# Channel attention, attention and a mixture of LoRA experts in one kernel: the tie test, the two features and the gates change engines

## The reference, cut to what matters

```python
# x: (16, 64, 2048); ctx_4096: (16, 1601, 2048)
x = x + xattn(layernorm(x), ctx_4096, conv_w, gamma, beta)
x = x + attn(layernorm(x), wq, wk, wv, wo)          # causal, 64 tokens, 32 heads, 8 KV heads
x = x + ffn(layernorm(x), gate_w, base_w, base_b, lora_A, lora_B)

def xattn(x, channel_map, ...):      # the part that the change touches
    k = 38                           # of C = 64 channels of x
    # top_k of channel_map over its 1601 channels, at each of the 16 x 2048 places;
    # the mask keeps those of the winners whose index is under 64
    mask = zeros(B, L, C).at[b, l, topk_idx].set(1)
    top, rest = mask * x, (1 - mask) * x
    c_max, c_avg = max(top, C), mean(top, C) * C / k
    s_max, s_avg = max(rest, C), mean(rest, C) * C / (C - k)
    A1 = sigmoid(relu(norm(conv7([c_max, c_avg]))))   # norm over all places, one channel
    A2 = sigmoid(relu(norm(conv7([s_max, s_avg]))))
    return top * A1 + rest * A2
```

## Time and profile before

| | |
|---|---|
| median of 3 runs | 2323.5 us (2322.08 to 2328.86) |
| the profiled execution | 2331.43 us, of which its span is 2329.6 |
| busy in the span | PE 2017.3 (87%), PEld 1656.8 (71%), DVE 1423.9 (61%), ACT 1011.1 (43%), POOL 979.4 (42%) |
| DMA | 407.69 MB, mean 175 GB/s |
| the costliest lines | L1744 to L1746 PE 742.5, 727.5 and 727.3; L1198 POOL 653.8; L440 DVE 521.7; L680 PE 462.7; L641 ACT 416.6 |

### The profile page before, as it was taken

How to read it: one execution, slowest core, us unless ns; L and a number is a source line. 1 busy time by engine, 2 the same in 40 slices (tenths; PEclk the granted TensorE clock), 3 DMA queues, 4 the chain that set the end, 5 groups by cost and what they waited for, 6 DMA issues and landing times. The chain is left out here.

```text
span 2329.6 us, 39066 instructions
## 1 busy us (share of the span) xinstructions
PE 2017.3 (87%) x15210; PEld 1656.8 (71%) x15210; DVE 1423.9 (61%) x2320; ACT 1011.1 (43%) x2006; POOL 979.4 (42%) x866
## 2 busy tenths in 40 slices
PE   4777788677762946999999999999999999999999
PEld 4566565566662935777787888887778878877887
DVE  6999899999999989744444530144445525731111
ACT  7777777777760136432332332232223322422222
POOL 1221121222214531665564555556555435634554
PEclk9999899999985968999999999999999999999999
DMA  9999787899960104542225443322244446333443
GB/s 381 369 359 326 273 302 268 299 327 336 336 215 17 73 19 127 158 127 82 76 84 181 136 142 116 100 80 76 82 152 143 136 127 214 124 109 124 144 144 119
DMA packets 150088, 407.69 MB, mean 175 GB/s; under 512 B 15376, under 2 KB 36112, under 8 KB 148112
## 3 DMA queue, kind: packets, MB, share of 16 engines
q1 hardware_dynamic: 149616, 403.55, 51.0%
q0 software_dynamic: 288, 1.64, 0.2%
HBM read 379.96 MB, written 25.17 MB: 174 GB/s over the span
## 5 line engine op out<-in xcount | busy, mean ns | idle before, releaser
L1198 POOL TENSOR_TENSOR t<-t,t 128x512 fp32r<-128x512 f32 (+1 forms) x488 | 653.8, 1351 | 680.9 <-ACT t L1191 680.5
L1744 PE MATMUL ps<-t,t 128*128 128x512 f32 x1856 | 742.5, 400 | 19.7 <-POOL t L1198 9.5
L1745 PE MATMUL ps<-t,t 128*128 128x512 f32 x1856 | 727.5, 392 | 0.0
L1746 PE MATMUL ps<-t,t 128*128 128x512 f32 x1856 | 727.3, 392 | 0.0
L680 PE MATMUL ps<-t,t 128*128 128x128 bf16 (+1 forms) x6656 | 462.7, 226 | 199.9 <-DVE t L440 185.3
L680 PEld LDWEIGHTS ps<-t,t 128*128 128x128 bf16 x6656 | 405.1, 103 | 292.8 <-DVE t L440 250.3
L1191 ACT ACTIVATE t<-t 128x512 fp32r<-128x512 f32 (+1 forms) x488 | 295.8, 608 | 712.4 <-PE ps L1746 393.1
L440 DVE TENSOR_SCALAR t<-t,t 128x1601 bf16<-128x1601 f32 x512 | 521.7, 1063 | 3.8 <-PE ps L680 0.3
L641 ACT ACTIVATE t<-t,t 128x1601 bf16<-128x1601 f32 x256 | 416.6, 1627 | 74.1 <-DVE t L582 70.6
L1744 PEld LDWEIGHTS ps<-t,t 128*128 128x128 f32 x1856 | 350.9, 189 | 100.2 <-issue 13.2
L1746 PEld LDWEIGHTS ps<-t,t 128*128 128x128 f32 x1856 | 351.1, 189 | 75.2
(11 more groups left out here) (212 smaller groups left out, 1684.2 us busy)
## 6 DMA issues: line engine op xcount, KB each, us to landing
t<-ctxT SPq DMA_DIRECT2D x256, 800.5 KB, 6.2
t<-wqkv SPq DMA_DIRECT2D x192, 256.0 KB, 3.2
t<-wo SPq DMA_DIRECT2D x128, 256.0 KB, 4.6
t<-wb SPq DMA_DIRECT2D x128, 256.0 KB, 3.4
t<-xT SPq DMA_DIRECT2D x32, 256.0 KB, 7.0
t<-xT SPq DMA_DIRECT2D x2, 4096.0 KB, 12.2
t<-x1d SPq DMA_DIRECT2D x32, 256.0 KB, 4.8
x2d<-t SPq DMA_DIRECT2D x32, 256.0 KB, 2.0
```

The costliest lines, as they stand in the source:

```text
L1198: e.tensor_tensor(wlo[r][:, 0:nk, :], raw[r][:, 0:nk, :], wh[r][:, 0:nk, :].bitcast(F32), ALU.subtract).then_inc(w_lo, 1)
L1744: e.matmul(bank[:, :], wh[r][:, q, :], xl, start=(kt == 0), stop=False)
L1745: e.matmul(bank[:, :], wlo[r][:, q, :], xh, start=False, stop=False)
L1746: m = e.matmul(bank[:, :], wh[r][:, q, :], xh, start=False, stop=(c == NCH[p] - 1 and q == nk - 1))
```

## The change

1. **Ties.** The two neighbour comparisons per quad leave VectorE. GpSimd subtracts neighbours instead, one instruction of 28 elements for a quad (`quad_gpsimd`), queued behind its copy of the quad's last tile. The flag is then "the smallest difference is zero" (`fin_vector` step 8 takes a minimum, `flags_vector` step 2 compares with zero). VectorE's `copy_predicated` and step 8 wait for GpSimd's `tied`.
2. **The layernorm's reciprocal** goes from the first to the late call of `ln0_vector` in its round.
3. **Setup.** The warming instruction of GpSimd is a `tensor_tensor` and no longer a `partition_all_reduce`; the gate weights land in another buffer, and GpSimd's copies don't wait for `gate_lo`.
4. **`ln0_out_gpsimd`**, the first six: they wait until the last mask of the search is written.
5. **Statistics.** `LAG` is 3 and no longer 4. The maxima are written straight into the padded feature tile `Yp`. The sums of batches 12 to 14 go from VectorE to TensorE: eight matmuls of 384 columns (eight channels x 48 rows of places) behind the 64 of batches 0 to 7, and one VectorE reduction over the eight. Batch 15 stays on VectorE. ScalarE takes the sums of batches 0 to 7 out of PSUM.
6. **Convolution and gates.** ScalarE writes the scaled top average and the two edges, VectorE the rest average; the centre tap (3) comes first. The relu and a Sigmoid are done on ScalarE, which writes `A2` itself; VectorE is left with the scale and one subtraction.

The diff, cut to its core (unused semaphores and renamed buffers left out):

```diff
 def setup_gpsimd(e):
-    e.partition_all_reduce(fl2[:, 0:2], fl2[:, 2:4], 128, ReduceOp.max).then_inc(warm, 1)
+    e.tensor_tensor(fl2[:, 2:4], fl2[:, 0:2], fl2[:, 0:2], ALU.subtract)
...
 def ln0_vector(e, i, late):
-            if i == LN0_VAR[h] + 1 and not late:
+            if i == LN0_VAR[h] + 1 and late:
                 e.wait_ge(ln0_std, h + 1)
                 e.reciprocal(ln0_rs[h][:, :], Mn[:, :]).then_inc(ln0_rstd, 1)
...
 def bounds(half):
-    e.tensor_tensor(eqb[y][:, two, :], v8[:, y, two, 0:7], v8[:, y, two, 1:8], ALU.is_equal).then_inc(tied, 1)
...
+def quad_gpsimd(e, i):
+    e.wait_ge(maxed, 4 * i + 4)
+    e.tensor_tensor(eqb[y][:, four, :], v8[:, y, four, 0:7], v8[:, y, four, 1:8], ALU.subtract).then_inc(tied, 1)
...
 def rows_gpsimd(e):
     gather_gpsimd(e, 0, d_first[0])
+    e.wait_ge(masked, NMASKS)
     for j in range(6):
         ln0_out_gpsimd(e, j)
...
-    LAG = 4
-    BY_ACT, BY_DVE = range(8, 12), range(12, 16)
+    LAG = 3
+    BY_ACT, BY_PE, BY_DVE = range(8, 12), range(12, 15), range(15, 16)
+    late_sums = ps[4][:, 0:8 * NT * len(BY_PE)].rearrange("p (c n) -> p c n", c=8)
...
 def stats_vector(e):
         for b in range(B - LAG, B):
-            total(b)
+            if b in BY_DVE:
+                total(b)
             rest(b)
+        e.wait_ge(sums8, 2)
+        e.tensor_reduce(row_sums[:, 12:15, :], over_t(late_sums), AX.X, ALU.add).then_inc(v_sums, 1)
...
 def stats_tensor(e):
+        e.wait_ge(crucial, BY_PE.stop)
+        src = crc16[:, BY_PE.start - HB:BY_PE.stop - HB, :, :].rearrange("p b t c -> p c b t")
+        for k in range(8):
+            m = e.matmul(late_sums.rearrange("p c (b t) -> p c b t", t=NT), ident, src[:, 8 * k:8 * k + 8], start=(k == 0), stop=(k == 7))
...
 def conv_vector(e):
-        for s in range(2):
-            do(e.tensor_scalar(Z[:, s, :], Z[:, s, :], sc[:, 12 + s:13 + s], w16[:, 14:15], ALU.mult, ALU.mult))
-        do(e.tensor_scalar(Z[:, :, :], Z[:, :, :], w16[:, 15:16], 0.0, ALU.add, ALU.max))
-        e.wait_ge(z_exp, 1)
-        do(e.tensor_scalar(Zt[:, :, :], Zt[:, :, :], 1.0, None, ALU.add))
-        do(e.reciprocal(A12[:, :, :], Zt[:, :, :]))
-        do(e.tensor_tensor(Dm, A12[:, 0, :], A12[:, 1, :], ALU.subtract))
-        e.tensor_copy(A2, A12[:, 1, :]).then_inc(gates, 1)
+        e.tensor_scalar(sc[:, 14:16], sc[:, 12:14], w16[:, 14:15], None, ALU.mult).then_inc(z_scale, 1)
+        e.wait_ge(z_out, 4)
+        e.tensor_tensor(Dm, A1[:, :, :], A2, ALU.subtract).then_inc(gates, 1)
...
 def conv_scalar(e):
+        e.activation(feature[2], row_sums, ACT.Copy, scale=PART[0]).then_inc(f_in, 1)
+        for x_, cols in ((0, slice(0, 3)), (1, slice(19, 22))):
+            e.wait_ge(conv_edges, x_ + 1)
+            e.activation(Yp[:, :, cols], edge[x_], ACT.Copy).then_inc(f_edge, 1)
...
+            e.activation(Zt[:, s, :], Z[:, s, :], ACT.Relu, scale=sc[:, 14 + s:15 + s], bias=w16[:, 15:16]).then_inc(z_out, 1)
+            e.activation((A1[:, :, :], A2)[s], Zt[:, s, :], ACT.Sigmoid).then_inc(z_out, 1)
```

More of the change, by code:

```diff
@@ L259, in build @@
     crc_off = 96 * KB
-    crc = [at(crc_off + i * 4 * KB, [NT, C]) for i in range(HB, B)]
+    crc16 = at(crc_off + HB * 4 * KB, [B - HB, NT, C])
     crc8 = at(crc_off, [HB, NT, C])
@@ L468, in fin_vector @@
             if s == 8:
-                i = e.tensor_reduce(flg[:, b, :], eqb[y][:, :, :], AX.X, ALU.max)
+                e.wait_ge(tied, 4 * (b + 1))
+                i = e.tensor_reduce(flg[:, b, :], eqb[y][:, :, :], AX.X, ALU.min)
             i.then_inc(fin, 1)
@@ L596, in search_vector @@
                 e.wait_ge(a_dec, g + 1)
-                e.wait_ge(tied, 2 * g + 2)
+                e.wait_ge(tied, g + 1)
                 w = insA[:, 4 * g:4 * g + 4].rearrange("p (a n) -> p a n", n=1).to_broadcast([128, 4, 3])
@@ L661, in search_scalar @@
                         counts_scalar(e, i, v)
+    def quad_gpsimd(e, i):
+        b, t0 = tile_of(4 * i)
+        y, four = b % 2, slice(t0, t0 + 4)
+        if b >= 2 and t0 == 0:
+            e.wait_ge(fin, NF * (b - 1))
+        e.wait_ge(maxed, 4 * i + 4)
+        e.tensor_tensor(eqb[y][:, four, :], v8[:, y, four, 0:7], v8[:, y, four, 1:8], ALU.subtract).then_inc(tied, 1)
     def search_gpsimd(e):
-        e.wait_ge(gate_lo, 1)
         for n in range(B * NT):
@@ L835, in build @@
     crucial, rest_set, rest_max = sem("crucial"), sem("rest_set"), sem("rest_max")
-    crucial_sum, sums8, v_sums = sem("crucial_sum"), sem("sums8"), sem("v_sums")
-    LAG = 4
-    BY_ACT, BY_DVE = range(8, 12), range(12, 16)
+    crucial_sum, sums8, v_sums, top_max = sem("crucial_sum"), sem("sums8"), sem("v_sums"), sem("top_max")
+    LAG = 3
+    BY_ACT, BY_PE, BY_DVE = range(8, 12), range(12, 15), range(15, 16)
+    sums_out = sem("sums_out")
+    feature = [Yp[:, B * f:B * f + B, 3:19] for f in range(4)]
+    row_sums = stat[:, 2, :, :]
+    late_sums = ps[4][:, 0:8 * NT * len(BY_PE)].rearrange("p (c n) -> p c n", c=8)
     def xn_of(b):
@@ L862, in stats_vector @@
             e.wait_ge(crucial, b + 1)
-            e.tensor_reduce(stat[:, 0, b, :], crc_of(b), AX.X, ALU.max)
+            e.tensor_reduce(feature[0][:, b, :], crc_of(b), AX.X, ALU.max).then_inc(top_max, 1)
             if b >= LAG:
@@ new lines, in conv_vector @@
+        e.wait_ge(z_out, 4)
+        e.tensor_tensor(Dm, A1[:, :, :], A2, ALU.subtract).then_inc(gates, 1)
+    def conv_tensor(e):
+        e.wait_ge(f_in, 2)
+        e.wait_ge(rest_max, B)
+        e.wait_ge(top_max, B)
+        e.matmul(edge[0], cst[:, C_SHL:C_SHL + 128], Yp[:, :, 16:19], start=True, stop=True).then_inc(conv_edges, 1)
+        e.matmul(edge[1], cst[:, C_SHR:C_SHR + 128], Yp[:, :, 3:6], start=True, stop=True).then_inc(conv_edges, 1)
+        e.wait_ge(z_part, 1)
+        e.wait_ge(f_edge, 2)
@@ L969, in build @@
+        for s in range(2):
+            e.wait_ge(z_out, s + 1)
+            e.activation((A1[:, :, :], A2)[s], Zt[:, s, :].rearrange("p (b t) -> p b t", t=NT), ACT.Sigmoid).then_inc(z_out, 1)
     row_gates, row_gates_v, gated = sem("row_gates"), sem("row_gates_v"), sem("gated")
```

108 lines of the change are left out of this document (54 added, 54 removed).

## The result

The changed kernel takes 2313.6 us, the median of 11 runs (2308.41 to 2317.76). The kernel before, run beside it, takes 2322.8 us (11 runs, 2319.43 to 2328.86). The ratio is 0.9959 with an interval of 0.9948 to 0.997: 9.2 us faster, between 7 and 12. The forecast was 2310, in a range of 2299 to 2321, with faster as the likeliest. That is 13.7 us under the kernel before where 9.2 were measured. The profiled execution took 2312.61 us, span 2310.4.

A forecast was written before the change was run, and what follows sets the result against it. VectorE was taken to pace the search, the DMA its first 100 us, and TensorE all from 918 us. -8 + 1.3 - 5.7 + 4.9 - 6.2 = -13.7 us gave 2310 against the median, range 2299 to 2321.

The forecast's parts named there:

- the forecast case: Whole kernel: the main outcome, forecast at 2310 us with its own range 2305 to 2315; chance 0.50.
- ties, with GpSimd's part: Search: two short VectorE instructions fewer per quad, -8 us; GpSimd's 64 small differences cost 1.3 us.
- reciprocal: Search: masks ahead of the reciprocal remove both VectorE waits for ScalarE's square root, 5.7 us less; bounds 4.9 and 5.7.
- end of the search: Last masks: freed of GpSimd's products, 8.4 us, partly lent as `fin_vector` instructions are held; net 2.5 us less, bounds 2.5 to 8.4.
- row of sums to feature: TensorE's late sums: wide matmuls add 10.5 us; convolution starts 4.9 us later, with the 2.5 us saved earlier already included.
- feature to gates: Convolution and gates: shorter work on VectorE and ScalarE saves 6.2 us in sum; bounds 4 and 7.
- part 3: Setup at the kernel's start: gains nothing, since the start is bound by the transfer.
- Nothing holds `fin_vector`: Rival, end of the search: the last masks give 8.4 us and not 2.5, total 2304 us; chance 0.12.
- Wide matmuls at 0.117: Rival, late sums: TensorE's wide matmuls run at 0.117 us per 128 columns, total 2305 us; chance 0.12.
- DMA takes the ties' gain: Rival, search: the DMA takes back the 8 us of the ties' removal, total 2318 us; chance 0.15.
- GpSimd's port: Rival, search: each of 64 small differences holds a mask by a fixed time; at 0.35 us, total 2331; chance 0.07.
- The pick waits for `tied`: Rival, search: GpSimd's difference comes late, stuck behind a copy, so VectorE's pick waits; chance 0.01.

The follow-up runs named there:

- e_ties_dve: The changed kernel with the two tie comparisons per quad back on VectorE and GpSimd's differences gone: 2320.84 us, ratio 0.9992 to the kernel before.
- e_recip_early: The changed kernel with the layernorm's reciprocal back ahead of the first masks of its round: 2316.25 us, ratio 0.9972 to the kernel before.
- the first profile: The kernel before, unchanged, in the profiled execution from which the forecast was made: 2331.43 us.
- e_before_again: The kernel before, unchanged, run once more for a second profile: 2325.16 us in the profiled execution.
- e_no_mask_wait: The changed kernel without the wait for the last mask in front of GpSimd's first six products: 2323.55 us, ratio 1.0008 to the kernel before.
- e_wide_consecutive: The changed kernel with the wide matmuls' moving operand read as consecutive elements (sums of batches 12 to 14 not the reference's): 2310.69 us, one run.
- e_ties_four: The changed kernel with four 28-element differences per quad on GpSimd instead of one, 192 more: 2313.84 us, ratio 0.9955 to the kernel before.

## Why the prediction was right, and where it was off

The steps all went the ways that were forecast, by the mechanisms that were forecast save for the reciprocal's, and 2313.6 us lies inside the forecast case's own range of 2305 to 2315. But of the 13.7 us forecast only 9.2 came (7 to 12), and that the total is this near is in part luck: the reciprocal and the end of the search gave up to 4.8 us less than forecast, the ties and the gates about 2 more. By the steps, in us:

| step | forecast | measured |
|---|---|---|
| ties, with GpSimd's part | -6.7 | -8.3 in the trace, -7.2 by medians (e_ties_dve) |
| reciprocal | -5.7 | -2.7 (e_recip_early) |
| end of the search | -2.5 | -2.7 against the first profile, -0.7 against the second |
| row of sums to feature | +7.4 | +7.8 and +7.6 |
| feature to gates | -6.2 | -6.9 in both |
| sum | -13.7 | -12.8, and -11.0 |

The sums are those of the column with the first and the second profile's terms. The medians say -9.2 (7 to 12). In the traces TensorE's last stage starts at 906.2 against 917.8 and 919.0. That is 11.6 and 12.8 earlier, 2 to 4 us more than the medians; the same search ended over a spread of 3 us, which is as much. No run takes part 6 back: the 6.9 of the gates rest on the rows of one stage, alike against both profiles.

**The ties.** Right in size, with a term too many. GpSimd's differences cost some 0.4 us at most, so the 1.3 us charged for them is too much. I had said that the first 100 us would give nothing, as the DMA bounds them; but the changed kernel is 2 us ahead already in round 12, at 124.2 us against 126.2 and 126.9. The DMA share is 1.01 there, at 388 GB/s where it was 384 and, in e_before_again, 383: the tiles came a little sooner. Whether the faster VectorE brought that about isn't settled, since other executions with GpSimd's differences reach that round at up to 126.0, and e_ties_dve without them at 126.3.

**The reciprocal.** This is the step that was mis-sized: 5.7 forecast with bounds of 4.9 and 5.7, and 2.7 measured. Both waits vanished, as the prediction said, but it took it that nothing is late next. Late next is ScalarE's readout L651, queued behind the same square root: 1.84, 0.69 and 0.42 us at the picks of rounds 25, 26 and 37. I asked what lies ahead of the reciprocal on VectorE, and not what lies behind the square root on ScalarE. The waits for TensorE's counts, in rounds 15 to 18 and 27 to 30, are no part of this: they were there before, at 5.7 us, and are 6.3 now.

**The last masks.** Three `fin_vector` instructions were held as forecast, and the net against the first profile is 2.7. But the bounds of 2.5 to 8.4 left out what the second profile shows: the kernel before pays less when GpSimd's load of code ends later against the masks, and then the gain is 0.7. On the other side stands what e_no_mask_wait showed. Setup's instruction, "nothing" in part 3, removes the load of code (e_ties_dve shows it gone) that had kept the products away from the small picks; part 4's wait takes over that service. Part 3 without part 4 loses the 10 us again, and in the first profile of the kernel before the last small pick (702.99 to 703.17) was clear of the products (703.70) by 0.5 us.

**Late sums.** 16 x 384 x 1.72 ns = 10.5 us is what the trace shows, to the hundredth; the reduction was 0.56 and not 0.6, and the feature starts 0.56 us behind it. e_wide_consecutive shows that choosing the row by its step was what made it right: L881 and L1143 have the same type and shape, and only their steps differ.

**Convolution and gates.** 20.5 us against the 21 forecast. The Sigmoid starts 0.02 us after its table load ends (853.12 + 1.28, then 854.42), as the square root had the earlier trace rows. The drain that the Trainium skill, "ScalarE: Activation LUTs", on what ACT_TABLE_LOAD costs, adds to the load is in neither row.

**The rivals.** Nothing holds `fin_vector`: refuted, 2.27 us each. Wide matmuls at 0.117: refuted (10.50 us). DMA takes the ties' gain: refuted, waits of 15.4 against 15.7 us, and e_ties_dve is 7.2 us slower. GpSimd's port: refuted by e_ties_four with the fourfold, at 1.2 us for 192 more. The pick waits for `tied`: no such wait in the trace.

## What to carry to other kernels

When a wait is taken away, look at the queue of the engine that was waited for: whatever stands behind the awaited instruction there is as late as before, and the next reader of it inherits the wait. Before work is put on an engine "that is idle", add it to the end of its own row: TensorE had 3.8 us of slack for 10.5 us of matmuls, and taking them off again gave 6.6 us. An instruction of another engine that only warmed something up may be what kept two engines out of each other's way; if it goes, say what keeps the order now.

## What was not expected of the hardware

- VectorE's masks and small GpSimd instructions share without loss to VectorE: 28 elements took GpSimd 0.23 us at least and mostly about 1.0 in e_ties_four, while five masks kept 4.91 us. With 1024-element products it goes both ways: products last 3.09 and not 2.34 us with masks between them, and each mask 3.13 and not 1.05.
- A 4-element VectorE instruction that began during GpSimd's gather took 14.82 us, through six products that followed the gather at once. With the products 11 us later it took 0.18 us at the same place in the gather, and among products 2.27 us. The cause is open.
- TensorE at a granted clock of 1.00: 384 f32 columns took 0.656 us at a step of 64 elements and 0.334 us consecutive.
